# A macaron block with two mixture-of-experts FFNs: the second FFN's tokens routed and scattered in two parts, padding rows written in long runs

## What is computed

```python
x = x + 0.5 * ffn(layernorm(x), w_router, w1, b1, w2, b2)
x = x + attn(layernorm(x), ...)          # gated recurrent attention, 8 heads of 64
x = x + 0.5 * ffn(layernorm(x), w_router, w1, b1, w2, b2)

def ffn(x, w_router, w1, b1, w2, b2):    # 8 experts, 128 -> 512 -> 128, top 1
    probs = softmax(x @ w_router)
    sel = argmax(probs); wgt = probs[sel]
    for e in range(8):
        h = relu(x @ w1[e] + b1[e])
        out += (sel == e) * wgt * (h @ w2[e] + b2[e])
```

## Time and profile before

| | us |
|---|---|
| three runs, median (lowest to highest) | 521.03 (519.73 to 521.4) |
| the profiled execution | 517.26 |
| its span, first to last instruction | 515.4 |
| TensorE busy | 396.6 (77%) |
| VectorE busy | 318.1 (62%) |
| ScalarE busy | 216.2 (42%) |
| GpSimd busy | 189.9 (37%) |
| mean granted TensorE clock | 0.905 of full speed |

### The profile page before, as it was taken

The page is one execution under the profiler, slowest core; times in us unless marked ns, Lnnn a source line. Parts: engine busy times, 40 slices in busy tenths (PEclk is TensorE's granted clock), DMA queues, the critical chain, the costliest instruction groups (busy, mean ns, idle before and its releaser), DMA issues.

```text
span 515.4 us, 9840 instructions
## 1 busy us (share of the span) xinstructions
PE 396.6 (77%) x2994; PEld 329.1 (64%) x2995; DVE 318.1 (62%) x963; ACT 216.2 (42%) x555; POOL 189.9 (37%) x171
## 2 busy tenths in 40 slices
PE   4439699916999889898989998898998850079980
PEld 4413599904777668676767776686777840079980
DVE  3561577767357788278785577892887435047763
ACT  2530344424455473364545455734556311034430
POOL 4256045521004432314554054323145524714550
PEclk9999999966999997999999999989999555579995
DMA  8999222130000000000000000000004000112215
GB/s 277 227 398 201 46 64 72 56 97 2 0 1 1 3 1 0 1 0 0 0 0 0 1 0 0 0 0 0 1 2 163 1 1 26 51 47 68 68 54 169
DMA packets 26107, 27.06 MB, mean 52 GB/s; under 512 B 2945, under 2 KB 23041, under 8 KB 25697
## 3 DMA queue, kind: packets, MB, share of 16 engines
q1 hardware_dynamic: 22002, 17.98, 13.6%
q0 software_dynamic: 2496, 5.13, 3.4%
q10 hardware_dynamic: 1584, 3.63, 2.0%
HBM read 17.52 MB, written 9.21 MB: 52 GB/s over the span
## 4 chain that ended last, share of the span: by engine, by line
issue 31%; PE 26%; POOL 21%; DMA 10%; DVE 9%; ACT 2%; POOLq 0%; SPq 0%; ACTq 0%; DVEq 0%
PE bank L777 23%; POOL slots L471 6%; POOL HS L497 4%; DMA slots<-QKT 4%; POOL W1R L500 4%; POOL W1R L498 3%; POOL W1R L503 2%; DMA slots<-XN,POS 2%; POOL LA L484 2%; DMA QKT<-by_token 1%; PE bank L856 1%; DMA WR<-w_router 1%; DMA by_token<-YB,IDX 1%; DMA XB<-slots 1%; DVE W1R L1574 1%
## 5 line engine op out<-in xcount | busy, mean ns | idle before, releaser
L497 POOL TENSOR_TENSOR HS<-HS,MHALF 128x8 f32<-128x8 f32 x16 | 26.3, 1645 | 114.1 <-DVE HS L1584 114.1
L477 POOL DMA_INDIRECT by_token<-YB,IDX x46 | 44.0, 956 | 65.3 <-DVE YB L1291 64.7
L777 PE MATMUL bank<-XBT,W1R 128*128 128x128 f32 x368 | 52.7, 290 | 0.0
L672 ACT ACTIVATE WVT<-bank,AC 128x128 f32<-128x128 f32 x128 | 36.6, 375 | 36.1 <-PE bank L777 36.1
L777 PE MATMUL bank<-W,HT 128*128 x368 | 49.1, 277 | 0.0
L777 PEld LDWEIGHTS bank<-XBT,W1R 128*128 128x128 f32 x368 | 48.0, 204 | 0.7 <-ACT XBT L580 0.3
L777 PEld LDWEIGHTS bank<-W,HT 128*128 128x128 f32 x368 | 45.3, 194 | 0.3
L471 POOL DMA_INDIRECT slots<-XN,POS x32 | 31.9, 996 | 28.8 <-DMA slots<-QKT 11.7
L580 ACT ACTIVATE XBT<-bank 128x128 f32<-128x128 f32 x46 | 12.8, 278 | 62.8 <-PE bank L856 40.8
L856 PE MATMUL bank<-K,XB 128*128 128x128 f32 x46 | 13.7, 299 | 32.9 <-DMA XB<-slots 32.8
L636 ACT ACTIVATE QKT<-bank,COLS 128x512 f32<-128x512 f32 x32 | 22.0, 689 | 38.9 <-PE bank L777 38.9
(11 more groups left out here) (289 smaller groups left out, 1015.2 us busy)
## 6 DMA issues: line engine op xcount, KB each, us to landing
W<-w SPq DMA_DIRECT2D x2, 2048.0 KB, 8.2
slots<-QKT SPq DMA_DIRECT2D x2, 1483.5 KB, 21.0
XB<-slots SPq DMA_DIRECT2D x46, 64.5 KB
W<-w SPq DMA_DIRECT2D x1, 2064.0 KB
QKT<-by_token SPq DMA_DIRECT2D x8, 256.0 KB, 3.7
X<-x SPq DMA_DIRECT2D x4, 256.0 KB, 6.0
out<-X SPq DMA_DIRECT2D x4, 256.0 KB, 2.5
by_token<-YB,IDX POOLq DMA_INDIRECT x46
```

Of the source, the lines that this page charges most:

```text
L477: g.indirect_dma_start(out=by_token[f], out_offset=bass.IndirectOffsetOnAxis(ap=IDX[:, j:j + 1], axis=0), in_=YB[:, j, :], in_offset=None) ...
L497: step.do(g.tensor_tensor(HS[:, 3, :], HS[:, 2, :], MHALF[:, 0:H], ALU.pow))
L672: ins = a.activation(DT[:, hf, m, :], DM[:, m * P:(m + 1) * P], ACT.Exp, bias=AC[:, c, h:h + 1])
L777: return t_.matmul(o, l, r, start=start, stop=stop, skip_group_check=True)
```

## The change

The first FFN, the attention's arithmetic and the 23 blocks of both FFNs stay. New constants: EARLY = 12 tiles, AHEAD = 5 blocks, REGION = 16 blocks to an expert.

**Two parts of the routing.** The first 12 tiles are routed inside the last chunk: their logits go to bank 1 between the steps of PE (all three wait until ACT has copied the second transposes out of that bank), DVE makes their one-hot (`early_choice`) and, after `variance(b, 3)`, their rows (`early_route`) and a first block table (`early_blocks`). For rows to be known before the counts are complete, every expert has a region of 16 blocks of its own in slots[1], which now has 146 blocks and two to fill up (it is written as 37 transfers of 512 rows from FILL1). 12 tiles of 128 tokens over 8 experts hold at least 5 full blocks; these five come first in the new table. The last four tiles follow in `late_route`, with ranks from short bf16 matmuls. A block's place in slots[1] is no longer k * 128 but a table entry (ROWNO), which SP reads into a register for each load. The index of a padding row is made by a minimum with a column of constants.

**Two parts of the scatter.** POOL scatters 12 tiles (`scattered_early`), with `rstd(1, 1)` in their middle, then four. SP waits for the block table and the first twelve for blocks 0 to 4, and for the rest before block 5.

**Fills and loads.** The fill of slots[0] writes all 23 rows of a partition to one run of 11,868 bytes; the fill of slots[1] moves from the start to behind the first FFN, in runs of 2,064 bytes. ACT's four loads of L540 are issued after the first FFN's exponential.

```diff
-            sp.dma_start(slots[0].rearrange("(k p) w -> p k w", p=P), FILL).then_inc(slots_filled[0], 16)
+            sp.dma_start(slots[0].rearrange("(p k) w -> p k w", p=P), FILL).then_inc(slots_filled[0], 16)
...
-            sp.dma_start(slots[1].rearrange("(k p) w -> p k w", p=P), FILL).then_inc(slots_filled[1], 16)
...
                 if f == 1:
+                    for i in range(NFILL):
+                        rows = slots[1][i * FROWS * P:(i + 1) * FROWS * P, :]
+                        sp.dma_start(rows.rearrange("(p k) w -> p k w", p=P), FILL1[:, :, :]).then_inc(slots_filled[1], 16)
...
                 def load_block(k, j):
-                    sp.dma_start(XB[:, j, :], slots[f][bass.ds(k * P, P), :]).then_inc(xb_loaded[f][j], 16)
+                    if f == 1:
+                        row = sp.value_load(ROWNO[0:1, bass.ds(k, 1)], min_val=0, max_val=(NSLOT - 1) * P)
+                    else:
+                        row = k * P
+                    sp.dma_start(XB[:, j, :], slots[f][bass.ds(row, P), :]).then_inc(xb_loaded[f][j], 16)
...
                     sp.wait_ge(idx_copied[f], k + 1)
+                    if f == 1 and j == AHEAD - RING:
+                        sp.wait_ge(scattered[f], 16 * (NT - EARLY))
                     load_block(k + RING, j)
...
-                sp.wait_ge(scattered[f], 16 * NT)
+                if f == 0:
+                    sp.wait_ge(scattered[f], 16 * NT)
+                else:
+                    sp.wait_ge(eid_ready[f], 1)
+                    sp.wait_ge(scattered_early, 16 * EARLY)
...
+                    pool.wait_ge(pj_full, NB * NPJ)
+                    token_numbers(1)
+                    pool.wait_ge(slots_filled[1], 16 * NFILL)
+                    pool.wait_ge(pos_ready[1], 1)
+                    pool.wait_ge(xn_ready[1], EARLY)
+                    scatter(1, 0, EARLY // 2, scattered_early)
+                    rstd(1, 1)
+                    scatter(1, EARLY // 2, EARLY, scattered_early)
+                    pool.wait_ge(pos_ready[1], 2)
+                    pool.wait_ge(xn_ready[1], NT)
+                    scatter(1, EARLY, NT, scattered[1])
...
                 variance(b, 3)
+                if last:
+                    early_route()
                 update_x(b, 2)
+                if last:
+                    early_blocks()
                 gate(b, 3)
```

245 lines of the change are left out of this document (195 added, 50 removed).

## The result

| | before | after |
|---|---|---|
| runs, median (lowest to highest), us | 520.38 (517.38 to 521.4) | 502.16 (499.35 to 503.94) |
| the profiled execution | 517.26 | 503.94 |
| its span | 515.4 | 502.1 |
| TensorE busy | 396.6 | 395.7 |
| VectorE busy | 318.1 | 327.5 |

The ratio of the changed kernel to the one before is 0.9654, with a 95% interval of 0.9592 to 0.9717: 18 us faster, give or take 3. The forecast of 502.2 was met to a tenth. Much of that is luck. In the two profiled executions three terms of the sum were wrong: the start gained 3.7 us more than forecast, the attention lost 3.8 us that were forecast at nothing, and the routing gained 5.5 us less. That leaves 13.3 us of the 18.8 forecast, and what closes the gap in the medians is in no trace.

A forecast was written before the change was run, and what follows sets the result against it. POOL's sixteen indirect scatters, 1.28 us each, were taken to bound the second FFN's start. Gains of 3.4 us at the start and 15.4 at the second FFN sum to 18.8: 521.03 - 18.8 = 502.2, range 497.5 to 508.

The forecast's parts named there:

- Part 1: Start: the fill in long runs frees SP and POOL, SELQ starts 2.3 us earlier; 3.4 us gained, bounds 0 and 5.
- Part 2: Last chunk: early routing puts `centre` 1.6 us later and `gate(3)` 2.4 later; block table ready at 432.7, at most 434.4.
- (a): Last chunk: state decays, second transposes and two logit groups in front put `from_state` 2.2 us later, at 400.9.
- (b): Last chunk, PE: a third group of logits ahead of `values` costs 0.87 us.
- (c): Last chunk: `values` take 2.00 us instead of 3.03, as transposes and logits fill most of PE's quiet stretch.
- rival A: Last chunk: the clock falls before `values` all the same, `centre` 4.1 us later than forecast; 506.3 us, chance 0.2.
- (d): Last chunk, DVE: `early_choice` takes 1.3 us; behind `variance(3)` 26 operations take 6.4, POOL covering all but 0.9.
- Part 3: Second FFN: the twelfth scatter lands at 435.0, 2.3 us after the table; first `up` at 439.4, 15.4 us gained.
- B: Start gains nothing, because the fill still holds SP or the setup hangs on something else; 505.6 us, chance 0.12.
- C: Ring of blocks becomes bound by SP's register reads, costing 3.6 us over 18 blocks; 505.8 us, chance 0.1.
- D: DVE's routing holds up POOL's twelve early scatters; 529 us if each is stretched by 2.2, chance 0.03.
- E: Second FFN's first blocks still wait for all sixteen scatters or the table; gain 10, 511 us, chance 0.03.

The follow-up runs named there:

- r4: The changed kernel with the third group of early logits behind values on PE and `early_choice` behind the centre on DVE; ratio 0.967 to the kernel before.
- b1: The kernel before, unchanged, profiled once more; the kernel before took 516.8 us on that chip.
- s1: The kernel before with only the new start: both fills in long runs, slots[1]'s still at the start, ACT's four loads moved; ratio 0.994.
- s2: The kernel before with only the fill of slots[0] changed, to runs of 11,868 bytes; ratio 0.993.
- k1: The changed kernel with 13 unread transposes added on PE to fill two gaps in the last chunk; ratio 0.965 to the kernel before.
- s3: The kernel before with only ACT's four weight loads moved behind the first FFN's exponential; ratio 0.998.

## Why the prediction was right, point by point

**The total, 502.2**: right by luck in part, as the sum of terms that were not. Gained on average in the traces: 4 to 6 at the start (forecast 3.4), 11.2 at the routing (forecast 15.4), and some 3 given back in the attention (forecast nothing), which makes 12 to 14. The two pairs of profiled executions differ by 13.3 and 11.8 us, the medians by 18.2 and 17.2. The pairs are one-sided: both profiled executions of the changed kernel were the slowest of their runs (503.94 and 502.61 us), and those of the kernel before, 517.26 and 514.43, lay below its median. The last 3 to 6 us lie in executions of which there is no trace; fewer falls of the clock, as r4 had (10.2 us low instead of 20.4), would make up 2 to 3 of them, but this is argued and not shown.

**Part 1.** The rows up to SELQ were right, and so was the choice of the row of 21.05 us over the rule of 512 bytes. The step that was wrong is that the setup alone bounded the first blocks before: they also waited for a scatter that took 6.60 us to land beside the second fill, and in b1 for that alone. Nor were "the setup's later links" unchanged: the second group of fold matmuls took 3.78 us before and 1.99 after, which is the chance of one profile's clock. The forecast of 3.4 us for the start stands near what s1 and s2 gave in time, 2.9 and 3.7, but for another reason.

**Part 2**, counted from the third chunk's centre. (a) `from_state` was put at +2.2 and came +1.9 later. (b) The third logits took 1.75 instead of 0.87. (c) Values took 3.65 instead of 2.00. With these the centre is 3.5 us later and not 1.6: rival A, to which I gave 0.2, is what happened in every traced execution of the new routing, though at half its price: A had the centre 4.1 us behind the forecast, and it was 1.9. Its grounds, and the forecast's, were wrong too: the clock fell with the gaps filled (k1) and held through values behind a wait of PE in the old order (s1, s2). (d) Behind `variance(3)`, DVE's 26 operations took 8.7 us and not 6.4, of which 2.5 are the three that POOL's operations stretched; so POOL's `head_norm` covered all but 3.1 instead of 0.9. The gate came 6.6 us later than before, not 2.4.

**Part 3.** The table was no bound, as forecast: EID was written at 432.85, the twelfth scatter had landed when SP woke, at 434.68. The first scatter needed 0.5 us behind POOL's `head_norm` instead of 1.1, and with the centre's delay it was 1.3 late. Between the first and the twelfth lay 17.3 us instead of 15.7: the term for `rstd` left out that the variance would not be ready (2.24 us). From the twelfth to `up` I had 6.7, measured 6.68 to 9.32. These three, 1.3 + 1.6 + 0 to 2.6, are the whole miss of 2.7 to 5.5 us at `up` within 0.2 us.

**Rivals.** B: refuted. C: refuted, the blocks keep their period of 1.90 us (in after's chain their W1 matmuls follow at 446.88, 448.78, 450.68), and the stretch from `up` to the rows by token is 48.9 to 50.7 us with or without SP's reads. D: refuted as I put it; no early scatter took longer than 1.40 us. But the same neighbours hurt the other way round: POOL's tensor operations held up DVE's, which I had not looked for. E: refuted, the first load left at 437.15 and the last of the sixteen scatters at 437.36. **The fills**: at no cost, as forecast.

## What to carry to other kernels

Before a wait is taken away, list what else ends at nearly the same time: at the start there were two (a slow landing and the setup), and which one bound changed from execution to execution, and at the scatter, work that "POOL covers" was longer than the cover by the time it shared with POOL. Count from a common point late in the program when parts are compared; from there two executions of one kernel agree to 0.15 us up to the twelfth scatter, where the whole times of one kernel's runs spread over 4 to 6. And an address that must be read from a table belongs ahead of the wait that it would otherwise stand behind.

## What the hardware did that I had not expected

- A DVE product or cast on SBUF that began while a POOL tensor operation of 512 elements ran ended with it: 1.04, 0.93 and 1.23 us for operations of 0.25 us size, in eight of the nine profiles of the changed routing (in r4 other ones were caught, with 1.18, 0.93 and 0.93); reductions and operations that read PSUM beside them kept their 0.25. Beside POOL's power of 8 elements (L535) two operations with both inputs in SBUF were not held, 0.29 us each; one of them, beside the first operation of 512 elements in r4, took 1.18.
- SP's read of a number into a register and the instructions behind it cost between 0.8 and 3.4 us for the first two loads; where it was more than 0.8, the chain has pieces of about 0.7 us.
- The granted clock falls once in most sequences of the attention, for what shows as 3.4 or 6.8 us at half speed, mostly about a sequence after the fall before it (a few stand elsewhere: after's at 166, r4's at 307), and keeping PE busy ahead of it did not prevent it (k1). A fall of 6.8 us costs 1.5 us between two centres.
- A fill of 1.48 MB in pieces of 516 bytes takes 19 to 21 us as the first at the start (16.0 with four loads moved away) and 35.9 as the second (s3). The last scatter beside it lands in 4.4 to 8.0 us instead of 2.3. In runs of 11,868 bytes a fill takes 10 to 11 us.
